# A graph network step on one core: one-hots of two pairs made by one VectorE instruction, and a tile's bytes spread nine pairs behind its first

## The reference

```python
edge_index = jnp.stack([src, dst])          # row = src, col = dst
def step(h, _):
    messages = h[col] @ W_msg.T + b_msg
    agg = segment_sum(messages, row)        # 3125 nodes
    gi = agg @ W_ih.T + b_ih
    gh = h @ W_hh.T + b_hh
    r = sigmoid(i_r + h_r); z = sigmoid(i_z + h_z)
    n = tanh(i_n + r * h_n)
    return (1.0 - z) * n + z * h, None
x = layernorm(x + h_after_5_steps)
```

## Time and profile before

| | us |
|---|---|
| median of three runs | 626.7 (624.03 to 627.04) |
| the profiled execution's own time | 625.54 |
| its span in the profile | 623.7 |
| PE busy | 579.6 (93% of the span) |
| DVE busy | 341.8 (55%) |
| ACT busy | 321.6 (52%) |
| chain that ended last: PE | 76% of the span |
| chain that ended last: DMA | 8% |

### The profile page before, as it was taken

How to read it: one execution, slowest core, us unless ns; L and a number is a source line. 1 busy time by engine, 2 the same in 40 slices (tenths; PEclk the granted TensorE clock), 3 DMA queues, 4 the chain that set the end, 5 groups by cost and what they waited for, 6 DMA issues and landing times.

```text
span 623.7 us, 8646 instructions
## 1 busy us (share of the span) xinstructions
PE 579.6 (93%) x3090; PEld 327.9 (53%) x3090; DVE 341.8 (55%) x726; ACT 321.6 (52%) x574; POOL 285.8 (46%) x398
## 2 busy tenths in 40 slices
PE   4799988889998999999999999999999999999991
PEld 3565655554454555556545555655555654555550
DVE  5769999997477323346523234642323662354466
ACT  3568888877345344544444334633444544544352
POOL 5012222221301666764567764376566555666600
PEclk9779999999999999999999999999999999999996
DMA  6024655665000000000000000000000000000012
GB/s 169 24 61 117 124 119 123 123 119 83 1 1 2 1 0 1 0 1 0 1 2 0 1 1 1 1 0 1 0 2 0 1 2 0 1 0 1 2 42 64
DMA packets 32221, 18.56 MB, mean 30 GB/s; under 512 B 4657, under 2 KB 31256, under 8 KB 32176
## 3 DMA queue, kind: packets, MB, share of 16 engines
q1 hardware_dynamic: 29050, 13.91, 10.6%
q0 software_dynamic: 1856, 3.90, 2.4%
q10 hardware_dynamic: 1270, 0.16, 0.2%
HBM read 2.84 MB, written 1.60 MB: 7 GB/s over the span
## 4 chain that ended last, share of the span: by engine, by line
PE 76%; DMA 8%; DVE 7%; ACT 4%; issue 3%; SPq 1%; POOL 0%; DVEq 0%; ACTq 0%
PE PS L772 39%; PE PS L749 8%; PE PS L753 8%; DMA A<-stage 6%; PE PS L586 4%; PE PS L760 4%; PE PS L759 4%; PE PS L690 4%; ACT spread L985 2%; PE PS L681 2%; SPq L478 1%; ACT stage L973 1%; DVE y L1183 1%; DMA bmsg<-in_L_gnn_b_msg 1%; DVE parts L1142 1%
## 5 line engine op out<-in xcount | busy, mean ns | idle before, releaser
L545 POOL CAST ring<-A 128x896 f16<-128x896 uint8 (+4 forms) x324 | 249.7, 811 | 195.5 <-PE PS L772 182.4
L772 PE MATMUL PS<-ring,parts 128*128 128x448 f16 x1372 | 270.8, 352 | 2.0 <-DVE parts L1142 2.0
L772 PEld LDWEIGHTS PS<-ring,parts 128*128 128x128 f16 x1372 | 133.6, 98 | 128.2 <-issue 10.7
L1343 DVE SCALAR_TENSOR_TENSOR pre_n<-PS,small,gate_r 128x448 f32<-128x448 f32 x35 | 23.9, 683 | 207.2 <-PE PS L760 207.1
L1036 ACT ACTIVATE ring<-A 128x896 f16<-128x896 uint8 (+4 forms) x144 | 105.8, 773 | 0.1
L1019 ACT ACTIVATE gate_r<-PS,small 128x448 f32<-128x448 f32 x35 | 22.2, 634 | 145.2 <-PE PS L753 145.2
L690 PE MATMUL PS<-spread,parts 128*128 128x448 f16 x294 | 71.9, 352 | 9.7 <-ACT spread L985 9.5
L985 ACT ACTIVATE spread<-A 128x1056 f16<-128x1056 uint8 (+1 forms) x75 | 70.8, 949 | 16.2 <-DMA A<-stage 16.2
L536 POOL DMA_DIRECT2D A<-stage x50 | 26.7, 534 | 105.5 <-ACT stage L973 105.5
L681 PEld LDWEIGHTS PS<-hot_row,hot_key 128*128 128x128 bf16 x588 | 45.8, 127 | 26.7 <-ACT stage L973 13.6
L749 PE MATMUL PS<-hT,wT 128*128 128x448 f32 x140 | 58.6, 541 | 0.0
(11 more groups left out here) (148 smaller groups left out, 490.0 us busy)
## 6 DMA issues: line engine op xcount, KB each, us to landing
A<-stage SPq DMA_DIRECT2D x150, 66.0 KB, 3.3
A<-stage POOLq DMA_DIRECT2D x50, 66.0 KB, 3.0
y<-in_x SPq DMA_DIRECT2D x3, 256.0 KB, 6.5
y<-in_x SPq DMA_DIRECT2D x2, 384.0 KB
out<-y SPq DMA_DIRECT2D x4, 192.0 KB, 2.3
out<-y SPq DMA_DIRECT2D x3, 256.0 KB, 2.2
edges_dst<-in_dst SPq DMA_DIRECT2D x1, 195.3 KB
w_raw<-in_L_gnn_W_ih SPq DMA_DIRECT2D x1, 192.0 KB
```

The lines of the kernel that those rows point to most:

```text
L545: last = nc.gpsimd.tensor_copy(to, data)
L772: mm = pe.matmul(PS[:, AGG_BANKS[(t * LEGS + b) % 2], 0:LW], parts[:, k, part, :], ring[:, SLOT_OF[at_piece] % SLOTS, k % 2, :], start=(k ...
```

## The change

Three edits, all in the counting stage.

1. `one_hots` is called 50 times with d instead of 100 times with p. One `hot_key` instruction (1536 numbers) and one `hot_row` instruction (1320) make what two made before, for pairs 2d and 2d+1. The three slots hold two pairs each, so six pairs instead of three lie between DVE and PE. DVE waits for both pairs of the slot to be counted, and PE for the whole double. The last tile's `hot_row` is made with all five columns a pair instead of three.
2. In DVE's order `hot_high` and `hot_low` of the next tile stand behind a tile's first double (before: behind its third pair), and the low halves stand behind the double of their pair.
3. `SPREAD_AT` goes from 7 to 9 and `USE_AT` from 9 to 11: the spreads of a tile, and the products that read them, come two pairs later in ACT's and PE's order.

```diff
-SPREAD_AT, USE_AT = 7, 9
+SPREAD_AT, USE_AT = 9, 11
...
-        hot_key = counting.next("hot_key", [P, HOTS, P, KEYS], BF16)
-        hot_row = counting.next("hot_row", [P, HOTS, COLS, CW], BF16)
+        hot_key = counting.next("hot_key", [P, HOTS, 2, P, KEYS], BF16)
+        hot_row = counting.next("hot_row", [P, HOTS, 2, COLS, CW], BF16)
...
-                    pe.wait_ge(hots_ready, p + 1)
+                    pe.wait_ge(hots_ready, p // 2 + 1)
+                    slot = p // 2 % HOTS
...
-                def one_hots(p):
-                    k, q = divmod(p, PT)
-                    n = COLS if p < FULL_PAIRS else len(COLS_OF[0])
-                    if p >= HOTS:
-                        dve.wait_ge(counted, p - HOTS + 1)
-                    nc.vector.tensor_tensor(hot_key[:, p % HOTS, :, :], iota_key,
-                                            keyT[:, p, :].unsqueeze(1).to_broadcast([P, P, KEYS]), ALU.is_equal)
-                    if q == 0:
+                def one_hots(d):
+
+                    k, half = divmod(d, 2)
+                    if d >= HOTS:
+                        dve.wait_ge(counted, 2 * (d - HOTS) + 2)
+                    nc.vector.tensor_tensor(hot_key[:, d % HOTS, :, :, :], iota_key.unsqueeze(1).to_broadcast([P, 2, P, KEYS]),
+                                            keyT[:, 2 * d:2 * d + 2, :].unsqueeze(2).to_broadcast([P, 2, P, KEYS]), ALU.is_equal)
+                    if half == 0:
                         dve.wait_ge(factors_made, 3 * (k + 1))
...
-                    if (k + 1, q) == (TILES_SOONER, HOTS - 1):
-                        dve.wait_ge(slots_kept_too, 3)
-                    if k + 1 < KT and q == HOTS - 1:
+                    if k + 1 < KT and half == 0:
+                        if k + 1 == TILES_SOONER:
+                            dve.wait_ge(slots_kept_too, 3)
+                        if k:
+                            dve.wait_ge(hots_ready, d)
                         high_and_low(k + 1)
-                    if k + 1 < KT and q == PT - 1:
+                    if k + 1 < KT and half == 1:
                         high_times_value(k + 1)
 
-                for p in range(PAIRS):
-                    one_hots(p)
-                    if 1 <= p < 1 + UNITS - LOWS_SOONER:
-                        low_part(0, LOWS_SOONER + p - 1)
+                for d in range(PAIRS // 2):
+                    one_hots(d)
+                    for p in range(2 * d - 1, 2 * d + 1):
+                        if 1 <= p < 1 + UNITS - LOWS_SOONER:
+                            low_part(0, LOWS_SOONER + p - 1)
```

More of the change, by code:

```diff
@@ L106, in gnn_kernel @@
     assert DR * DW == E and 2 * KLAST == P and WIN > 2 * REPEAT and WIN == 2 * P + HALF and 2 * HALF == P
-    assert PAIRS <= P and GLAST == PT and FB * BANKS == NP
+    assert PAIRS <= P and PAIRS % 2 == 0 and PT == 4 and GLAST == PT and FB * BANKS == NP
     with ExitStack() as ctx:
@@ L681, in count @@
                             mm = pe.matmul(PS[:, COUNT_BANKS[p % 2], side * CW:(side + 1) * CW],
-                                           hot_key[:, p % HOTS, :, 3 * side + n], hot_row[:, p % HOTS, c, :],
+                                           hot_key[:, slot, p % 2, :, 3 * side + n], hot_row[:, slot, p % 2, c, :],
                                            start=(n == 0), stop=(n == 2))
@@ L1305, in one_hots @@
                         dve.wait_ge(factors_made, 3 * (k + 1))
-                    highs = hot_high[:, k % 2, q * COLS:q * COLS + n, :, :]
-                    lows = hot_low[:, k % 2, q * COLS:q * COLS + n, :].rearrange("p c (b d) -> p c b d", d=DUP)
+                    n = 2 * COLS
+                    highs = hot_high[:, k % 2, half * n:half * n + n, :, :]
+                    lows = hot_low[:, k % 2, half * n:half * n + n, :].rearrange("p c (b d) -> p c b d", d=DUP)
                     nc.vector.tensor_tensor(
-                        hot_row[:, p % HOTS, 0:n, :].rearrange("p c (a b d) -> p c a b d", a=HIGH, d=DUP),
+                        hot_row[:, d % HOTS, :, :, :].rearrange("p h c (a b d) -> p (h c) a b d", a=HIGH, d=DUP),
```

## The result

| | before | changed |
|---|---|---|
| median, us | 624.58 (622.82 to 627.04, 8 runs) | 622.36 (621.48 to 625.2, 8 runs) |
| ratio to before | | 0.996, 95% interval 0.9941 to 0.9978 |
| a later comparison | 625.38 | 623.23 (12 runs), 0.996, 0.9942 to 0.9977 |
| profiled execution (span) | 625.54 (623.7) | 622.44 (620.6) |

The change makes the kernel faster by 0.4%: 2.2 us by the medians, where a gain of 8.4 us was forecast (625.54 to 617.1). The ratio is the same in both comparisons. In the profiled executions 3.1 us are gained.

What follows compares the result with a forecast made beforehand. The loop through ACT's copies and the stores was taken to bound the counting, DVE afterwards. Counting -9.0, start -0.5, tail +1.1 made -8.4 us: 617.1 from 625.54, 617.8 allowing for the median; range 614 to 623.5.

Steps and rivals of the forecast that it cites:

- The doubles on DVE: DVE in the counting: double hot_key 0.87 us, double hot_row 0.76, a tile 3.95 against 4.22.
- rivals 3 and 4: DVE: doubles save 0.15 us an instruction, 612.2, chance 0.06; doubled hot_key at half rate, about 651, chance 0.04.
- The first twelve pairs: Start of the counting: waiting for a whole double against fewer stops for low halves, -0.5 us.
- The pace: Counting from pair 12 to the last count: 4.02 us a tile, 88.65 us in all, -9.0 us.
- the round: Loop of ACT's copies and their stores, two tiles: closes at 7.25 us, 3.63 a tile instead of 4.58.
- the queue on SP at the last store: SP, from a tile's last copy to its last store's issue: shrinks from 1.6 us to 0.2.
- The signs named ahead: Profile after: SP's last store issued within 0.3 us of its copy, last count near 137 us, ACT's DMA waits well under 13.3.
- A change of less than 0.5%: Whole kernel: a time within about 3.1 us, 0.5%, of no change; chance 0.16.
- rival 1: Stores in the counting land later, 4.5 us throughout: pace 4.23, total 621.7 to some 622.3; chance 0.20.
- "The largest of" five limits: Counting pace a tile: largest of DVE 3.95, ACT 3.75, loop 3.63, PE 3.62, SP 3.59 us, plus 0.07.
- The tail: Behind the last count: three items of tile 22, six products on PE, move there, +1.1 us.
- Rival 2: ACT's new places gain nothing, loop holds 4.5 us a tile, DVE's saving idles: 626.5 to 627; chance 0.10.

Runs made afterwards that it cites:

- spread_only: Kernel before with only SPREAD_AT, USE_AT = 9, 11, one-hots still single; 622.33 us, ratio 0.9946 to the kernel before.
- stage12_pool4_low: Changed kernel with 12 stage buffers, POOL issuing four of eight stores a tile, and low halves moved between hot_key and hot_row; 614.27 us, ratio 0.9819 to before.
- extra_store: Changed kernel with two more 64 KB stores a tile, issued by POOL to rows nobody reads; 637.46 us, ratio 1.0187 to before.
- pool4: Changed kernel with POOL issuing four of a tile's eight stores instead of two, SP four; 619.86 us, ratio 0.9894 to before.
- all_use10: stage12_pool4_low with USE_AT 10 instead of 11, products one count sooner; 622.78 us, ratio 0.9959 to before.
- singles_stage12: Kernel before with single one-hots, SPREAD_AT, USE_AT = 9, 11 and 12 stage buffers; 621.53 us, ratio 0.9919 to before.

## Why the prediction was right and wrong

*The doubles on DVE.* Right to 0.01 us (0.87, 0.76, 3.94), and rivals 3 and 4 are gone: the fixed part saved is 0.07 us an instruction, and the doubled form keeps its rate. But DVE wasn't what the counting waited for, so this was worth nothing.

*The first twelve pairs.* Right in size. -0.5 was forecast; the double of pair 12 starts at 48.18 against 48.95, -0.77. In the profiled execution of the later comparison it starts at 48.74, so it varies by half a microsecond from one execution to the next:

```profile
48.18 0.96 DVE L1303 TENSOR_TENSOR hot_key<-iota_key,keyT 128x1536 bf16<-128x1536 bf16 x1
```

*The pace.* This is the term that failed. From pair 12 to the last count 141.72 - 48.18 = 93.54 us passed, 88.65 were forecast: 4.9 of the 5.3 us by which the profiled execution, 622.44, misses the sum of 617.1 (the tail adds 0.8, the start takes 0.3 off, what lies behind 0.1). The step that failed is the second half of the round: "the queue on SP at the last store has shrunk from 1.6 us to 0.2", with 3.3 us of landing behind it. The stretch from the last copy to the last landing, 5.41 us in the round of the earlier trace rows and 5.12 in the mean, was to come down to 4.08; it stayed, at 5.19. The reordering did what I wrote for ACT (3.75 us to 3.18 measured, 3.17 forecast), and that half alone makes the gain: (3.75 - 3.18) / 2 = 0.28 us a tile, against the 0.25 by which the pace fell. (3.18 + 5.19) / 2 = 4.19 is the pace within 0.04.

Two terms of that stretch were too small. The queue fell only from 1.67 to 1.14 us, not to 0.18, since I had laid out SP's issues at exactly 0.6 us each; in tile 13 two took 1.40 and 1.02. And the last store's landing, counted from the start of its issue, rose from 3.45 to 4.05 us, where I had kept the median of all stores, 3.3. I also read the earlier trace rows wrongly: the landing there includes the issue, so the queue before was 2.26 us and not 1.6, and my own layout should have closed at 3.35 + 3.3 = 6.65 us and not 7.25. Put right, that would have made the forecast of the round still lower, 3.33 us a tile, and the miss larger. The earlier trace rows had the warning: issues up to 1644 ns, landing up to 4.5 us. The signs named ahead fit this: SP's last store was to be issued within 0.3 us of its copy and came 1.14 us behind it, and the last count was to come near 137 and came at 141.72. A change of less than 0.5% had been given a chance of 0.16.

With 4.23 in place of 4.02 the sum is that of rival 1, 621.7 to 622.3, and 622.36 came. Rival 1 had the right direction of one term (the last store lands later, 4.05 us and not its 4.5) and kept the queue at 0.2. That its pace is the measured 4.23 is luck: a landing that is too long and an issue counted twice stand in it for the missing queue. The forecast's own number has a slip of 0.1: the middle of 617.1 and 618.3 is 617.7.

*"The largest of" five limits.* This was the second weakness. The pace was taken from DVE, which had the largest of the five figures, so an error of 0.6 us a tile in the round changed the limit itself. I took DVE's 3.95 as the bound since the round, at 3.63, seemed to have 0.3 us to spare. With the round at 4.23 DVE's gain is idle time: spread_only, without it, is as fast.

*The tail.* +1.1 forecast, +1.9 measured. Six products more stand there. For the other 0.8 there is PE's wait of 0.68 us ahead of its products at 143.20, for a stage copy; ACT's timeline has that copy behind a spread of tile 22:

```profile
141.88 1.09 ACT L986 ACTIVATE spread<-A 128x1056 f16<-128x1056 uint8 x1
142.85 0.29 ACT L974 ACTIVATE stage<-PS 128x132 int32<-128x132 f32 x1
```

The sixth spread left over is thus ahead of the last copy and not, as I had it, beside the seventh legs. The long run of late products, 46 of them, comes behind and hides nothing, since it stands behind the spread products on PE. I had called this "nothing".

*Rival 2* was half right: the old stretch of more than 5 us ahead of the same copy did stay. What it left out is ACT's shorter half, so the places gained 0.25 us a tile and not nothing.

*Open.* Why SP's issues stretch, and why the last store lands later once the stores come sooner, isn't settled, so it is not shown why the stretch stayed at 5.2 us. Long issues and landings happened before as well (1644 ns, 4.5 us) and come where the DMAs move 120 to 140 GB/s; I didn't separate the number of stores in flight from their rate.

## What to carry to other kernels

Where an engine waits for the last of several stores, don't rebuild that wait from the median issue and the median landing of one store. Measure it whole, over all tiles, from the last copy to the last landing, and keep the measured stretch in the sum until a run shows it shorter: 5.12 us from the kernel before and ACT's 3.17 would have given (3.17 + 5.12) / 2 = 4.15 us a tile, where 4.23 came and 4.02 was forecast. Before a faster engine is paid for, look for the next limit within 5% of it: here two limits lay at 4.22 and 4.23 us, so that the doubles were worth nothing, and 4.5 us as soon as the other one was loosened (another queue for half of the stores, and a third set of buffers). With the third set alone they were still worth nothing; the other queue alone was not tried with singles. A lead that grows while the next engine does not speed up (DVE's last `hot_key` at 134.03, the last count at 141.72) is the mark of it.

## What the runs showed of the hardware

- With stores of 66 KB from one place of the on-chip memory to another, as here, the DMAs moved 138 GB/s over 90 us with two stores a tile added; the highest of the stretches looked at, there and in stage12_pool4_low, was 143. The profile's DMA share is no measure of what is left: it was 1.11 at those 138 GB/s, and 0.60 at 138 GB/s in stage12_pool4_low.
- SP's median landing over the whole stage, counted from the start of the issue, was 4.6 us in extra_store, 3.7 in pool4, 3.4 in the changed kernel and 2.8 in all_use10. The shortest between 60 and 130 us was 2.4 to 2.6 in all of them. An issue on SP took 0.55 or 0.60 us in the median, single ones up to 2.15 (singles_stage12); on POOL 0.53, the longest 0.71.
- POOL's stores landed in 2.5 to 3.9 us (median 3.5) while DVE was 100% busy from 67 to 90 us in the changed kernel. The fastest kernel of the study had half of its stores issued by POOL.
